# A decoder layer on one core: all steps of head, period and tail in another order

## The reference, cut to what matters

```python
# 1. attention with feature maps, 16 heads of 64, 32 features
q_prime = exp((x @ Wq + bq) . wq_feat);  k_prime = exp((x @ Wk + bk) . wk_feat)
D_inv   = 1 / (q_prime . k_prime.sum(tokens) + 1e-6)
context = einsum('bnhf,bnhd->bhfd', k_prime, v)
x = layernorm(x + (q_prime . context * D_inv) @ Wproj + bproj)
# 2. cross attention, 16 heads of 8, softmax over the 64 context tokens of the batch
x = layernorm(x + softmax(Q K^T / sqrt(8)) V @ Wo + bo)
# 3. feed-forward, 128 -> 512 -> 128, ternary weights, norm inside
h = layernorm(gelu(x @ ternary(W_fc).T), ln_w, ln_b)
x = layernorm(x + h @ ternary(W_proj).T)
```

## Time and profile before

| what | value |
|---|---|
| median of 3 runs | 674.66 us (672.16 to 675.87) |
| the profiled execution | 671.15 us, of which 669.1 us is the span from first to last instruction |
| granted TensorE clock, mean | 0.993 |
| PE busy / weight loads | 634.0 us (95%) / 442.2 us (66%) |
| DVE / ACT / POOL busy | 551.9 (82%) / 433.4 (65%) / 453.7 us (68%) |
| instruction DMAs of queue q8 | 103 packets, 1.69 MB |
| HBM read and written | 16.88 and 4.19 MB, 31 GB/s over the span |

### The profile page before, as it was taken

How to read it: one execution, slowest core, us unless ns; L and a number is a source line. 1 busy time by engine, 2 the same in 40 slices (tenths; PEclk the granted TensorE clock), 3 DMA queues, 4 the chain that set the end, 5 groups by cost and what they waited for, 6 DMA issues and landing times.

```text
span 669.1 us, 30120 instructions
## 1 busy us (share of the span) xinstructions
PE 634.0 (95%) x13024; PEld 442.2 (66%) x13024; DVE 551.9 (82%) x1519; ACT 433.4 (65%) x749; POOL 453.7 (68%) x495
## 2 busy tenths in 40 slices
PE   9999999999999999999899999999999999988774
PEld 6766767676667667666666666676676667556453
DVE  1756688888888898888789888988988899797887
ACT  4536475848577684848658485766848487766352
POOL 3333144977769596777859676795968789787542
PEclk9999999999999999999999999999999999999799
DMA  8102012232522634162262416235241624231300
GB/s 336 33 18 37 33 36 50 46 93 44 96 67 42 119 40 98 34 113 50 55 105 38 93 40 110 53 49 107 42 99 34 113 50 61 55 67 35 65 33 33
DMA packets 102581, 45.55 MB, mean 68 GB/s; under 512 B 93105, under 2 KB 93490, under 8 KB 102322
## 3 DMA queue, kind: packets, MB, share of 16 engines
q1 hardware_dynamic: 102450, 43.63, 32.2%
HBM read 16.88 MB, written 4.19 MB: 31 GB/s over the span
## 4 chain that ended last, share of the span: by engine, by line
PE 48%; POOL 22%; DVE 10%; DMA 7%; issue 7%; ACT 5%; SPq 1%; POOLq 0%; DVEq 0%; ACTq 0%
PE bank L330 8%; DMA gT<-gs 5%; POOL gall L1077 5%; PE bank L347 5%; POOL gs L1082 5%; PE bank L320 4%; PE bank L428 4%; PE bank L443 4%; PE bank L400 3%; DVE st L841 3%; POOL rstd L1035 3%; POOL cs L1110 2%; POOL x2s L1096 2%; PE bank L287 2%; PE bank L497 1%
## 5 line engine op out<-in xcount | busy, mean ns | idle before, releaser
L330 PEld LDWEIGHTS bank<-Mh,GT 128*32 128x32 f32 x4096 | 110.6, 110 | 24.0 <-issue 18.2
L330 PE MATMUL bank<-Mh,GT 128*32 128x128 f32 x4096 | 126.1, 273 | 0.4 <-issue 0.3
L871 DVE TENSOR_REDUCE mx<-bank 128x8 f32<-128x512 f32 x128 | 78.2, 682 | 15.1 <-PE bank L400 15.1
L1077 POOL TENSOR_TENSOR gall<-gall,lnr 128x512 f32<-128x512 f32 x56 | 71.0, 1279 | 19.7 <-DVE st L841 19.7
L648 ACT ACTIVATE PT<-bank 128x512 f32<-128x512 f32 x128 | 64.6, 625 | 14.5 <-PE bank L428 14.5
L1035 POOL TENSOR_TENSOR rstd<-ve,mhalf 128x4 f32<-128x4 f32 x64 | 66.8, 1045 | 5.3
L347 PE MATMUL bank<-Cb,qT 128*64 128x128 f32 x1024 | 66.8, 273 | 0.0
L1082 POOL TENSOR_TENSOR gs<-gall,gs 128x512 f16<-128x512 f32 x56 | 64.1, 1165 | 1.4 <-ACT gs L685 1.4
L320 PE MATMUL bank<-kp,xs 64*128 64x512 f32 x256 | 64.0, 616 | 0.0
L820 DVE COPY GT<-bank 128x512 f32<-128x512 f32 x78 | 49.4, 676 | 16.9 <-PE bank L320 13.4
L535 ACT ACTIVATE Mrow<-bank 64x128 f16<-64x128 f32 x16 | 4.3, 270 | 84.4 <-PE bank L409 84.4
(11 more groups left out here) (192 smaller groups left out, 1647.1 us busy)
## 6 DMA issues: line engine op xcount, KB each, us to landing
xT<-in_xT SPq DMA_DIRECT2D x16, 256.0 KB, 3.5
xs<-in_x_nat SPq DMA_DIRECT2D x16, 256.0 KB, 3.9
cxT<-in_cxT SPq DMA_DIRECT2D x16, 256.0 KB, 3.7
out_y<-yo SPq DMA_DIRECT2D x15, 256.0 KB, 2.0
Qm<-in_Wvp SPq DMA_DIRECT2D x1, 1024.0 KB, 7.1
gT<-gs SPq DMA_TRANSPOSE x56, 3.3
gall<-in_Wff SPq DMA_DIRECT2D x1, 768.0 KB, 9.9
small<-in_small SPq DMA_DIRECT2D x1, 523.0 KB, 8.4
```

What stands on the lines that cost most here:

```text
L330: m = e.matmul(bk[32 * j:32 * j + 32, tile(g_)], GT[b % 4][:, tile(hh, 32)], Mh[:, tile(hh)], start=True, stop=True)
L871: e.tensor_reduce(mx[s % 2][:, c0:c0 + 8], bank[uses["score", s, i][0]][:, :].rearrange("p (n k) -> p n k", k=64), AX.X, ALU.max).then_inc ...
L1077: e.tensor_tensor(g[t][:, :], g[t][:, :], lnr[:, :], ALU.mult).then_inc(s_gs, 1)
```

## The change

All 1379 steps stay, with the same operations, but the three strings give them another order. In HEAD no step of block 0 is left but its `loadx`: the weights come first, and the DMAs are issued in another order (small1, WkT, WqT, x before; Wvp, small2, bv, small1, WqT, Wff, WkT, x after). PERIOD begins at another step, so its lags are larger, and block 0 now starts inside it (`k0@1`, `k1@1` at n = 1). In PERIOD, ACT empties 4 g, 4 c and ks (before: 3 g and 3 c); over the whole plan the steps marked "+" go from 107 to 159. On POOL, step `ap2` waits also until `stat` of the block before has read `x2s`'s place (`s_x2c`). The lines of TAIL are cut here to the last ones.

```diff
 HEAD = """
-wk wb wq k0@0 small1 k1@0 zeros WkT k2@0 WqT split@0 k3@0 q0@0 q1@0 ks@0 g0+@0 g1+@0 loadx@0 mh0 mh1 Wvp g2+@0 g3+@0 bv q2@0 small2 kst@0 Wff nbeta
-q3@0 gam biasA g4+@0 g5@0 split@1 xb@0 loadc@0 g6@0 g7@0 c0+@0 dT@0 c1+@0 loadx@1 loadx@2 c2+@0 c3@0 xw c4@0 c5+@0 c6@0 c7+@0 bias2 bc0@0 bc1@0 bc2@0
-bc3@0 csplit@0 bias3 sbar
+wb Wvp small2 nbeta bv wq small1 biasA bias2 WqT mh0 mh1 gam wk xw zeros bias3 Wff WkT loadx sbar
 """
 PERIOD = """
-k0 k1 down0@4 down1@4 k2 score0@2 split@-1 loadc score1@2 o0@1 o1@1 o2@1 o3@1 rows@2 st1@1 g0+ g1+ g2+ g3 ap2@3 down2@4 k3 down3@4 ab2@3 q0 prob0@2
-prob1@2 st3@4 ap1@1 ap3@4 c0+ c1 pv0@2 x1s@1 ab1@1 ks gs0@3 c2 gs1@3 pv1@2 stat@3 up0@3 up1@3 up2@3 up3@3 q1 gh0@3 oturn0@2 cs0@2 kst q2 cs1@2 oturn1@2
-q3 g4 g5 g6 gs2@3 gl0@3 g7 gh1@3 qproj@1 gl1@3 kproj@1 c3 dT c4+ c5 c6 gs3@3 c7+ proj0@2 csplit proj1@2 vproj@1 xb gh2@3 st2@2 gl2@3 bc0 loadx@-2 gl3@3
-gh3@3 bc1 bc2 bc3
+xb@2 o3@3 up0@5 st1@3 gs0@5 rows@4 down2@6 up1@5 ab2@5 down3@6 st3@6 stat@5 up2@5 up3@5 gl0@5 q0@2 k2@2 k3@2 q1@2 g0@2 g1@2 g2+@2 ap1@3 gs1@5 gh0@5
+prob0@4 prob1@4 x1s@3 g3+@2 cs0@4 g4@2 gh1@5 c0+@2 pv0@4 gs2@5 ks+@2 oturn0@4 c1@2 c2@2 pv1@4 q2@2 oturn1@4 cs1@4 vproj@3 ap3@6 gl1@5 proj0@4 down0@5
+q3@2 kst@2 split@1 kproj@3 gh2@5 proj1@4 c3@2 dT@2 c4@2 st2@4 g5+@2 gs3@5 g6+@2 g7@2 ab1@3 bc0@2 bc1@2 bc2@2 bc3@2 qproj@3 k0@1 down1@5 gl2@5 k1@1
+c5+@2 c6+@2 ap2@4 gl3@5 c7+@2 loadc@1 gh3@5 score0@3 score1@3 loadx o0@2 o1@2 o2@2 csplit@2
 """
 TAIL = """
...
- proj1@2 st2@2 down3@3 prob0@1 ap3@4 ab2@2 prob1@1 st3@3 ap2@2 pv0@1 flip3@2 pv1@1 oturn0@1 up0@2 oturn1@1 up1@2 up2@2 up3@2
-turn0+@2 stat@2 ap3@3 proj0@1 turn1+@2 proj1@1 st2@1 ab2@1 turn2@2 turn3+@2 down0@2 down1@2 ap2@1 down2@2 down3@2 flip3@1 up0@1 up1@1 up2@1
-up3@1 st3@2 stat@1 turn0+@1 ap3@2 turn1+@1 turn2+@1 turn3+@1 down0@1 down1@1 down2@1 down3@1 st3@1 ap3@1
...
+prob0@1 ap2@2 prob1@1 pv0@1 oturn0@1 flip3@2 pv1@1 up0@2 up1@2 up2@2 oturn1@1 turn0+@2 up3@2 stat@2 proj0@1 ap3@3 turn1+@2 proj1@1 st2@1 down0@2
+down1@2 turn2+@2 down2@2 turn3+@2 down3@2 ap2@1 flip3@1 st3@2 up0@1 ab2@1 up1@1 up2@1 stat@1 turn0+@1 up3@1 turn1+@1 ap3@2 down0@1 turn2+@1 down1@1
+down2@1 turn3+@1 down3@1 st3@1 ap3@1
 """
...
                 if s > 0:
                     w.wait_ge(s_x2T, 16 * s)
+                    w.wait_ge(s_x2c, s)
                 e.tensor_copy(x2s[:, 0:512], x[:, :]).then_inc(s_x2h, 1)
```

More of the change, by code:

```diff
@@ L45 @@
+q3@2 kst@2 split@1 kproj@3 gh2@5 proj1@4 c3@2 dT@2 c4@2 st2@4 g5+@2 gs3@5 g6+@2 g7@2 ab1@3 bc0@2 bc1@2 bc2@2 bc3@2 qproj@3 k0@1 down1@5 gl2@5 k1@1
+c5+@2 c6+@2 ap2@4 gl3@5 c7+@2 loadc@1 gh3@5 score0@3 score1@3 loadx o0@2 o1@2 o2@2 csplit@2
 """
 TAIL = """
-k0@1 k1@1 loadc@1 score0@3 o0@2 ap2@4 score1@3 ab2@4 kproj@2 o1@2 o2@2 o3@2 st1@2 rows@3 g0@1 g1@1 gs0@4 ap1@2 k2@1 down0@5 down1@5 up0@4 tw@1 up1@4
-x1s@2 gs1@4 down2@5 down3@5 stat@4 gl0@4 up2@4 up3@4 prob0@3 c0@1 c1@1 xb@1 k3@1 g2@1 g3@1 gs2@4 gl1@4 prob1@3 c2@1 gh0@4 pv0@3 qproj@2 ks+@1 pv1@3
@@ L54 @@
-turn0+@2 stat@2 ap3@3 proj0@1 turn1+@2 proj1@1 st2@1 ab2@1 turn2@2 turn3+@2 down0@2 down1@2 ap2@1 down2@2 down3@2 flip3@1 up0@1 up1@1 up2@1
-up3@1 st3@2 stat@1 turn0+@1 ap3@2 turn1+@1 turn2+@1 turn3+@1 down0@1 down1@1 down2@1 down3@1 st3@1 ap3@1
+ab2@6 o3@4 st1@4 xb@3 up0@6 gs0@6 up1@6 rows@5 down2@7 up2@6 down3@7 up3@6 q0@3 k2@3 stat@6 q1@3 gs1@6 st3@7 g0@3 g1+@3 q2@3 k3@3 gl0@6 ap1@4 prob0@5
+prob1@5 loadx@1 c0+@3 g2+@3 g3+@3 q3@3 pv0@5 c1@3 oturn0@5 pv1@5 gs2@6 gh0@6 gl1@6 split@2 oturn1@5 x1s@4 ks+@3 gh1@6 c2@3 cs0@5 cs1@5 c3+@3 g4@3
@@ new lines @@
+kst@3 vproj@4 kproj@4 gs3@6 g5@3 g6+@3 g7@3 c4+@3 dT@3 c5+@3 proj0@5 csplit@3 proj1@5 gh2@6 k0@2 st2@5 bc0@3 gl2@6 bc1@3 bc2@3 ap2@5 bc3@3 gl3@6 c6@3
+down0@6 k1@2 qproj@4 g0+@2 c7+@3 gh3@6 o0@3 score0@4 k2@2 k3@2 score1@4 g1@2 down1@6 gs0@5 ab2@5 gs1@5 down2@6 up0@5 up1@5 down3@6 up2@5 rows@4 up3@5
+q0@2 stat@5 o1@3 gh0@5 o2@3 gs2@5 o3@3 prob0@4 ap3@7 loadc@2 st1@3 prob1@4 gl0@5 ks@2 c0+@2 pv0@4 xb@2 st3@6 g2@2 g3@2 gh1@5 ap1@3 kst@2 kproj@3 q1@2
+split@1 q2@2 c1+@2 pv1@4 c2+@2 q3@2 g4+@2 ab1@4 oturn0@4 g5@2 tw@1 oturn1@4 x1s@3 cs0@4 gl1@5 g6@2 g7+@2 cs1@4 dT@2 c3+@2 c4@2 c5+@2 vproj@3 k0@1
@@ new lines @@
+ap3@6 proj0@4 gs3@5 proj1@4 csplit@2 loadc@1 st2@4 bc0@2 gh2@5 bc1@2 gl2@5 bc2@2 bc3@2 g0+@1 qproj@3 gl3@5 k1@1 c6+@2 gh3@5 c7+@2 ab1@3 o0@2 ap2@4
+o1@2 score0@3 score1@3 kproj@2 g1@1 o2@2 o3@2 st1@2 k2@1 ab2@4 rows@3 g2@1 up0@4 down0@5 up1@4 ap1@2 up2@4 down1@5 up3@4 down2@5 xb@1 down3@5 q0@1
+k3@1 x1s@2 prob0@3 gs0@4 stat@4 prob1@3 g3@1 gl0@4 g4@1 c0+@1 gs1@4 gs2@4 ks+@1 pv0@3 gs3@4 oturn0@3 gh0@4 pv1@3 gl1@4 oturn1@3 q1@1 qproj@2 g5+@1
+cs0@3 gh1@4 c1+@1 q2@1 score0@2 c2+@1 cs1@3 g6+@1 score1@2 down0@4 gh2@4 vproj@2 ab1@2 proj0@3 gl2@4 q3@1 proj1@3 rows@2 gl3@4 kst@1 st2@3 gh3@4
@@ new lines @@
+down1@4 c3+@1 dT@1 c4+@1 c5+@1 ap2@3 ab2@3 prob0@2 bc0@1 bc1@1 bc2@1 bc3@1 g7+@1 csplit@1 c6+@1 down2@4 down3@4 o0@1 st3@5 gs0@3 stat@3 ap3@5 up0@3
+up1@3 up2@3 up3@3 c7+@1 kproj@1 o1@1 o2@1 o3@1 st1@1 st3@4 ap1@1 gs1@3 prob1@2 gh0@3 gl0@3 gs2@3 pv0@2 pv1@2 oturn0@2 flip+@1 gh1@3 gl1@3 oturn1@2
+qproj@1 gs3@3 gl2@3 score0@1 gh2@3 score1@1 proj0@2 proj1@2 down0@3 gl3@3 down1@3 gh3@3 rows@1 st2@2 ap3@4 down2@3 down3@3 st3@3 ab1@1 vproj@1 ab2@2
+prob0@1 ap2@2 prob1@1 pv0@1 oturn0@1 flip3@2 pv1@1 up0@2 up1@2 up2@2 oturn1@1 turn0+@2 up3@2 stat@2 proj0@1 ap3@3 turn1+@2 proj1@1 st2@1 down0@2
```

## The result

The changed kernel is slower: 684.92 us (684.3 to 687.1, 4 runs) against 673.41 us (671.34 to 675.87, 4 runs) of the kernel before on the same chip, a ratio of 1.0175 with a 95% interval of [1.013, 1.022]. Its profiled execution has a span of 682.5 us, 13.4 more than before. The forecast was 669.6, and even the range (up to 682) doesn't hold it.

A forecast was written before the change was run, and what follows sets the result against it. PE, 95% busy, was taken to bound the kernel. Span 669.1 + 7.0 (head) - 10.5 (periods) - 1.5 (tail) = 664.1 us, plus 2.05 around it 666.2, scaled to a median of 669.6 us; range 661 to 682.

The forecast's parts named there:

- PE has the same steps, so only waits can go: On PE: its work stays the same, so the change can save only the 0.2 to 2.3 us of waiting per period.
- Periods, 37.7 us: Eleven periods between `rows` steps: mean falls from 38.65 to 37.7 us as waits go, 10.5 us less in all.
- (1): `down` on PE: spread out, it no longer waits for gT's transposing DMA, listed at 4.5 us in eight waits.
- (2): `proj1` on PE: it no longer needs the bank that ACT's `Kg` frees, listed at 3.1 us in eight waits.
- (3): Runs of `c` and `pv` on PE: fewer instruction-load cuts, half of their 3.3 us counted as gone.
- (4): Copies per period: ACT takes about three more, going from 26.7 to 28.6 us; DVE goes from 33.3 to 31.4.
- The head, 7.0 us: Start of the kernel: `k0` of block 0 starts near 24.7 us, losing 8.7 us, less 1.7 us the old head loses later.
- The tail, -1.5 us: From `rows` of block 13: 1.0 us less up to `o3` of block 15, and 0.5 us less from there.
- At nothing: Waits priced at zero: `s_x2c` in `ap2`, `x2T` for `up0`, and `dT` to `bc0` (2.3 us needed, 2.4 us cover).
- Rival A: Slower: `Dblk` comes late, so `bc0` and all behind it lose 1.0 us per period; 681.7 us, chance 0.20.
- C: Rival, better: the head costs 4.7 us and the period goes to 37.4 us; 664.0 us, chance 0.15.
- D: Rival: the instruction-load cuts only move to other boundaries; adds 1.5 us, counted inside the forecast, no chance of its own.

The follow-up runs named there:

- experiment 13: Changed kernel with only `g2` and `g3` exchanged in the period, so the second chain has two steps of the same row half: 695.56 us, ratio to before 1.0312.
- experiment 1: Changed kernel with the `g` steps of PERIOD in pairs of neighbours and `c5` ahead of `bc0`: 691.29 us, ratio to before 1.0274.
- experiment 6: Changed kernel with `g` in pairs, `g3` evicted by DVE, `ap2` ahead of `qproj`, and the old head: 683.67 us, ratio to before 1.017.
- experiment 10: Changed kernel with `g` in pairs, `g3` evicted by DVE, old head, `ap2` behind `c6`, `rows` ahead of `up0`: 684.76 us, ratio to before 1.0116.
- experiment 11: Changed kernel with the old head, all `g` one place later (`g4` to `g7` one chain) and `c4` behind `g7`: 696.32 us, ratio to before 1.0288.
- experiment 8: Changed kernel with its 25 filling matmuls ahead of `wb` instead of ahead of `wk`: 689.78 us, ratio to before 1.0269.
- experiment 12: Changed kernel with 60 filling matmuls ahead of `wb` and none ahead of `wk`: 690.77 us, ratio to before 1.0208.
- experiment 9: Changed kernel with evictions divided between ACT and DVE as in the kernel before: 710.36 us, ratio to before 1.056.

## Why the prediction was wrong

**The step that failed** is "PE has the same steps, so only waits can go". The steps are the same and their time is not. Two chains of 1.92 us per period became three of 1.91, 1.15 and 1.91: +1.13 us per period, +19.7 us in the kernel, which is more than all that the measured span lies above the forecast one (682.5 against 664.1). Rows 11 held the key: eight matmuls in 1.99 us, 0.25 each, while the page has a mean of 616 ns for one. I used that row as 0.5 us per step, as cover for `Dblk`, and didn't ask why four steps take so little or what three would take.

**Periods, 37.7 us.** The gain by waits was real and larger than forecast: over the ten periods 3.0 us less in spite of 11.3 us more of `g`, so 14.3 us less of all else, where 9.5 were forecast. Without the dearer `g` the period would be 38.42 - 1.13 = 37.3 us. But that is a sum and not a kernel, and by experiment 13 not all of a slot shows in the period (0.45 us in most, for 0.76). Four tries to have the new order with fewer slots (experiments 1, 6, 10 and 11) brought the gain back as late evictions and late x2T. That the broken chains give ACT and DVE the time that the new order needs is my reading of it, not tested by itself. By the prediction's own sign, a mean period over 38.2 us, it was wrong: 38.62 over eleven.

**Waits (1) and (2)** went as told. **(3)** too in the changed kernel's trace, but that was in part the luck of one execution: experiments 8, 12 and 13 have the same order around `c4` and show cuts of 1.3 to 1.9 us in it (by the distances between starts). **(4)** I weighed as a side effect; with the old division the new order is 25 us slower (experiment 9). DVE's 33.3 us of a period went to 32.5, ACT's 26.7 to 28.1.

**The head, 7.0 us.** The mechanism is right (`k0` inside the 23 to 26 us foretold but for 0.14), the term is mis-sized: 10.0 us at `o0` of block 0, 10.4 by the spans and about 8 by the ratios with the old head put back. `gam` is 1.3 us later than worked out: `wb` and `nbeta` took 4.1 us for the 3.4 allowed, `wq`, the biases and `mh` another 0.9, and PE began 0.3 earlier. By the trace of experiment 13 the same head can cost 2.7 us more. `k0` itself came 1.4 us late; 8.7 + 1.4 = 10.1, so of the 1.7 us that I took off for later losses of the old head nothing shows.

**"The filling of the pipe costs nothing"**: `rows` 0 to 1 took 1.6 us more; not tested by itself.

**The tail, -1.5 us.** From `rows` of block 13 it is -1.0. But `rows` 11 to 13, where the tail's list takes over, cost 5.6 us more, with `g` broken up there too (seven of the 18 slots belong to no full period); I had priced those two periods as steady ones.

**At nothing**: `bc0` never makes PE wait for `Dblk`, which ends 0.64 us ahead of it in the periods. The cover was 2.9 us and not 2.4, since the three `g` in it take 1.91 us and not 1.5: the row that I misread gave the room. Rival A, with its place there, is refuted; C's better period was there but for `g`; D's cuts were gone in this one trace. None of the rivals is what happened, and the forecast of slower by over 0.5%, 0.21, had the wrong mechanism. One reading of the earlier trace rows was loose: the first of the eleven periods lasts 37.10 us (36.63 busy, 790 matmuls), so 37.76 is the shortest of the other ten.
